# Graph result moved to channel order by TensorE selections into PSUM instead of DMA

## The reference, cut to what matters

```python
def _L2_conv_ref(x):                       # x already group-normalised
    X = x.reshape(Cs, N).T                 # nodes x 64 features
    A = (dist == 1) + eye
    sim = X @ X.T / (nrm[:, None] * nrm[None, :])
    m = (A + sim) * 0.5
    d = exp(diagonal(m) - logsumexp(m, axis=1))
    return relu(X * d[:, None])

def _L3_conv_ref(x, alpha, weight):
    a_bin = sign_ste(x - alpha[None])
    return conv2d(a_bin, sign_ste(weight), padding=1)      # 3 x 3, 64 -> 64

x = x + _L2_conv_ref(_gn(x))
x = x + _L3_conv_ref(_gn(x), alpha, weight)
```

## Time and profile before

| what | us |
|---|---|
| median of three runs | 321.22 |
| lowest and highest run | 321.09, 323.44 |
| the profiled execution's own time | 320.82 |
| its span, first to last instruction | 319.0 |
| TensorE busy in the span | 287.3 (90%) |
| VectorE busy | 270.7 (85%) |
| ScalarE busy | 167.6 (53%) |
| GpSimd busy | 119.3 (37%) |

### The profile page before, as it was taken

The page is one execution under the profiler, slowest core; times in us unless marked ns, Lnnn a source line. Parts: engine busy times, 40 slices in busy tenths (PEclk is TensorE's granted clock), DMA queues, the critical chain, the costliest instruction groups (busy, mean ns, idle before and its releaser), DMA issues.

```text
span 319.0 us, 6001 instructions
## 1 busy us (share of the span) xinstructions
PE 287.3 (90%) x2242; PEld 176.1 (55%) x2242; DVE 270.7 (85%) x415; ACT 167.6 (53%) x304; POOL 119.3 (37%) x163
## 2 busy tenths in 40 slices
PE   8698999599699999999999999479999999998895
PEld 8345988337354444567886644364344434367862
DVE  5799999797957599999988666976999999998673
ACT  1399553024250999940000004698888898999000
POOL 4004999982800669889996007000000000000000
PEclk9799999779799999999999999989999999999999
DMA  3421000000000000000000000363000000000603
GB/s 113 127 94 48 29 4 0 2 1 0 3 0 0 0 0 2 0 2 2 3 2 0 2 1 0 135 137 129 0 0 0 0 0 0 0 2 0 133 2 131
DMA packets 7613, 8.82 MB, mean 28 GB/s; under 512 B 2212, under 2 KB 5796, under 8 KB 7588
## 3 DMA queue, kind: packets, MB, share of 16 engines
q1 hardware_dynamic: 6260, 7.30, 7.5%
q10 hardware_dynamic: 1328, 1.18, 1.5%
HBM read 4.28 MB, written 2.10 MB: 20 GB/s over the span
## 4 chain that ended last, share of the span: by engine, by line
PE 64%; DVE 12%; issue 10%; ACT 8%; ACTq 3%; DMA 2%; DVEq 0%
PE ps L1376 15%; PE ps L1513 14%; PE ps L1390 9%; PE ps L1631 8%; PE ps L1527 6%; PE ps L1411 4%; ACT arena L891 3%; PE ps L1700 3%; ACT arena L874 2%; ACTq L389 2%; PE ps L1611 2%; DMA arena<-arena 2%; ACT arena L672 1%; DVE arena L1274 1%; DVE arena L1257 1%
## 5 line engine op out<-in xcount | busy, mean ns | idle before, releaser
L1631 PE MATMUL ps<-arena 128*128 (+1 forms) x256 | 63.3, 380 | 6.3 <-ACT arena L874 5.0
L874 ACT ACTIVATE arena<-ps 128x2048 f32<-128x2048 f32 x32 | 60.1, 1879 | 7.9 <-PE ps L1631 7.9
L1631 PEld LDWEIGHTS ps<-arena 128*128 (+1 forms) x256 | 24.3, 97 | 40.6 <-issue 14.1
L602 POOL TENSOR_TENSOR arena<-arena 128x768 f32<-128x768 f32 x21 | 40.1, 1940 | 4.8 <-ACT arena L777 4.6
L1257 DVE TENSOR_TENSOR arena<-arena 128x1024 f32 (+3 forms) x34 | 36.6, 1153 | 4.0 <-ACT arena L874 4.0
L1155 DVE TENSOR_TENSOR turns<-arena,ps 128x1024 f32<-128x1024 f32 x30 | 35.2, 1218 | 1.5 <-PE ps L1527 1.5
L1411 PE MATMUL ps<-ident 128*128 128x128 f32 x262 | 32.9, 287 | 3.3 <-DVE arena L1301 1.7
L1390 PE MATMUL ps<-arena 64*64 64x240 f32 (+3 forms) x576 | 31.2, 374 | 4.2 <-issue 2.6
L1376 PE MATMUL ps<-turns,k 128*128 128x512 f32 x80 | 34.8, 593 | 0.1
L1411 PEld LDWEIGHTS ps<-ident 128*128 128x128 f32 x262 | 31.9, 202 | 4.4 <-DVE arena L1301 1.9
L1513 PE MATMUL ps<-turns,shift 64*64 64x512 f32 x200 | 33.5, 592 | 0.0
(11 more groups left out here) (237 smaller groups left out, 506.6 us busy)
## 6 DMA issues: line engine op xcount, KB each, us to landing
scratch_x<-xs SPq DMA_DIRECT2D x4, 256.0 KB
arena<-arena SPq DMA_DIRECT2D x2, 512.0 KB, 3.3
out<-arena SPq DMA_DIRECT2D x4, 256.0 KB, 2.1
xs<-in_x SPq DMA_DIRECT2D x8, 64.0 KB
xs<-in_x ACTq DMA_DIRECT2D x8, 64.0 KB
arena<-arena SPq DMA_DIRECT2D x4, 128.0 KB, 3.4
arena<-arena ACTq DMA_DIRECT2D x4, 128.0 KB, 4.1
arena<-in_toep SPq DMA_DIRECT2D x1, 448.0 KB, 5.5
```

What stands on the lines that cost most here:

```text
L602: pool.tensor_tensor(out=view(folds[i % len(folds)], dx * 3 * PX, [(PX, 3), (1, PX)]), in0=view(hy, (by - dy) * W + (dy * 3 + dx) * PX, [( ...
L874: act.activation(E[k], ps[:, (k % 2) * 2048:(k % 2 + 1) * 2048], ACT.Exp, scale=0.5 / SPLIT ** 2, accum_out=rowsum[:, bass.ds(i, 1)]).then ...
L1631: ins = pe.matmul(bank(b0 + q), w, m[:, bass.ds(i * P + 512 * q, 512)], start=(t == 0), stop=(t == 1 and q > 0))
```

## The change

- `keep_nodes` uses Relu in place of Copy, so XT holds relu(X). The products xx, for the similarities, read the unrectified nodes from PSUM for all q.
- `scale_nodes` becomes one product of 1024 columns for each half. `add_back`, ScalarE's four scalings and the eight DMAs of `to_channels` go.
- A new `to_channels` on TensorE: for each half and each of two sources (x2R, then o2) 16 f32 matmuls, each with 32 columns of the identity (every fourth one, from t) as weights over all 128 partitions, 256 moving columns, and 32 partitions of PSUM as output. The two sources accumulate, so that x3 stands in channel order in two banks of each half: 0 and 1 for h=1, 2 and 3 for h=0. The addend's part is queued as soon as the far exponentials have left these banks; the other part waits for o2.
- The warm-up products between are replaced by 8 before the pair means of h=1; the 10 behind them stay.
- Statistics and signs read PSUM. The pair means move to bank 4+h and the convolution to banks 4 to 7.
- ScalarE moves each half of x3 from PSUM to x3S after the half's signs, for the last add, which waits for it.

```diff
-        o2, x3R = cut(0, 2048), cut(2048, 2048)
-
...
-        x3N = cut(16384, 2048)
+        o2, far_out = cut(0, 2048), cut(2048, 2048)
...
+        x3S = cut(16384, 2048)
...
+        def x3_bank(h, n=512):
+
+            return bank(2 * (1 - h), n)
+
+        def image_rows(b):
+
+            return view(x3_bank(b // 4), 64 * (b % 4), [(256, 4), (1, 64)])
...
-        def to_channels(eng, h, quarters):
-
-            for t in quarters:
-                eng.wait_ge(sem("x3_ready"), 4 * (1 - h) + t + 1)
-                eng.dma_start(view(x3N, h * 1024, [(256, 4), (1, 256)], 32 * t, 32),
-                              x3R[:, h * 1024 + t * 256:h * 1024 + (t + 1) * 256]).then_inc(sem(f"x3N_in{h}"), 16)
...
-            for h in (1, 0):
-                to_channels(sp, h, (0, 2))
...
-                act.activation(view(XT, q * 512, [(256, 2), (64, C4), (1, 64)]), nodes(ps, q), ACT.Copy).then_inc(sem("xt"), 1)
+                act.activation(view(XT, q * 512, [(256, 2), (64, C4), (1, 64)]), nodes(ps, q), ACT.Relu).then_inc(sem("xt"), 1)
...
-                    act.activation(x3R[:, c:c + P], ps[:, c:c + P], ACT.Exp, scale=0.5 / SPLIT ** 2,
+                    act.activation(far_out[:, c:c + P], ps[:, c:c + P], ACT.Exp, scale=0.5 / SPLIT ** 2,
...
-            act.wait_ge(sem("scale_ready"), 1)
-            for q in (3,):
-                for u in range(4):
-                    act.activation(o2[:, 256 * q + 64 * u:256 * q + 64 * u + 64], XT[:, 512 * q + 64 * u:512 * q + 64 * u + 64],
-                                   ACT.Copy, scale=Ssum[:, 4 * u + q:4 * u + q + 1]).then_inc(sem("scaled"), 1)
-            for h in (1, 0):
-                to_channels(act, h, (1, 3))
             for h in (1, 0):
                 root(rstd[:, 4 * h:4 * h + 4], pvar[:, 4 * h:4 * h + 4])
+                act.wait_ge(sem("apad"), 8 - 4 * h)
+                act.activation(x3S[:, 1024 * h:1024 * h + 1024], x3_bank(h, 1024), ACT.Copy).then_inc(sem("x3_kept"), 1)
...
                     dve.wait_ge(sem("xt"), q + 1)
-                    src = view(XT, q * 512, [(256, 2), (64, C4), (1, 64)])
-                else:
-                    src = nodes(ps, q)
-                dve.tensor_tensor(out=view(xx, q * 512, [(256, 2), (64, C4), (1, 64)]), in0=src,
+                dve.tensor_tensor(out=view(xx, q * 512, [(256, 2), (64, C4), (1, 64)]), in0=nodes(ps, q),
...
-            def scale_nodes(h, q, n):
-
-                dve.tensor_tensor(out=view(o2, h * 1024 + 256 * q, [(256, n), (64, 4), (1, 64)]),
-                                  in0=view(XT, h * 256 + 512 * q, [(512, n), (64, 4), (1, 64)]),
-                                  in1=view(Ssum, 16 * h + q, [(1, n), (4, 4), (0, 64)]), op=ALU.mult).then_inc(sem("o2_ready"), n)
-
-            def add_back(h, q):
-
-                c = h * 1024 + 256 * q
-                dve.scalar_tensor_tensor(out=x3R[:, c:c + 256], in0=o2[:, c:c + 256], scalar=0.0,
-                                         in1=view(x2R, h * 1024 + 64 * q, [(256, 4), (1, 64)]), op0=ALU.max,
-                                         op1=ALU.add).then_inc(sem("x3_ready"), 1)
+            def scale_nodes(h):
+
+                dve.tensor_tensor(out=view(o2, h * 1024, [(256, 4), (64, 4), (1, 64)]),
+                                  in0=view(XT, h * 256, [(512, 4), (64, 4), (1, 64)]),
+                                  in1=view(Ssum, 16 * h, [(1, 4), (4, 4), (0, 64)]), op=ALU.mult).then_inc(sem("o2_ready"), 1)
 
             def statistics(h, first, n):
 
-                dve.wait_ge(sem(f"x3N_in{h}"), 64)
+                dve.wait_ge(sem("x3_ready"), 2 - h)
                 for b in range(4 * h + first, 4 * h + first + n):
-                    dve.bn_stats(stats[:, 6 * b:6 * b + 6], image_rows(x3N, b)).then_inc(sem("moments"), 1)
...
-                link(dve.tensor_copy(pav, bank(h, 8)))
...
-                                      view(x3N, 1024 * h + 64 * b, [(256, 4), (16, 4), (1, 16)]), limit[:, b:b + 1], 0.5,
+                                      view(x3_bank(h), 64 * b, [(256, 4), (16, 4), (1, 16)]), limit[:, b:b + 1], 0.5,
...
-            dve.wait_ge(sem("x2R_in"), 16)
-            scale_nodes(1, 0, 1)
-            for q in range(4):
-                if q < 3:
-                    scale_nodes(1, q + 1, 1)
-                dve.wait_ge(sem("o2_ready"), q + 1)
-                add_back(1, q)
-            scale_nodes(0, 0, 3)
-            dve.wait_ge(sem("o2_ready"), 7)
-            for q in range(3):
-                add_back(0, q)
-            dve.wait_ge(sem("scaled"), 4)
-            add_back(0, 3)
+            scale_nodes(1)
+            scale_nodes(0)
...
                 dve.wait_ge(sem("l3_done"), i + 1)
+                dve.wait_ge(sem("x3_kept"), i // 2 + 1)
                 dve.tensor_tensor(out=view(yout, q * 512, [(PX, 2), (64, 4), (1, 64)]),
-                                  in0=view(x3N, 1024 * (q // 2) + 128 * (q % 2), [(64, 2), (256, 4), (1, 64)]),
-                                  in1=view(bank(2 + q), 0, [(PX, 2), (64, 4), (1, 64)]), op=ALU.add).then_inc(sem("y_ready"), 1)
+                                  in0=view(x3S, 1024 * (q // 2) + 128 * (q % 2), [(64, 2), (256, 4), (1, 64)]),
+                                  in1=view(bank(4 + q), 0, [(PX, 2), (64, 4), (1, 64)]), op=ALU.add).then_inc(sem("y_ready"), 1)
...
-                pe.matmul(bank(h, 8), pair_mean, mv[:, 8 * h:8 * h + 8], start=True, stop=False)
-                pe.matmul(view(bank(h), 1, [(2, 4)]), pair_mean, pstat[:, 4 * h:4 * h + 4], start=False,
+                pe.matmul(bank(4 + h, 8), pair_mean, mv[:, 8 * h:8 * h + 8], start=True, stop=False)
+                pe.matmul(view(bank(4 + h), 1, [(2, 4)]), pair_mean, pstat[:, 4 * h:4 * h + 4], start=False,
...
-            pe.wait_ge(sem("col_summed"), 5)
-            warm_up(14, 4)
-            for quarter in (2, 4, 6, 8):
-                pe.wait_ge(sem("x3_ready"), quarter)
-                warm_up(8, 4)
+            def to_channels(h, src, u, first):
+
+                for t in range(4):
+                    for q in range(4):
+                        ins = pe.matmul(view(x3_bank(h), 256 * t, [(1, 256)], 32 * q, 32), view(ident, t, [(4, 32)]),
+                                        view(src, 1024 * h + q * (64 if first else 256), [(u, 4), (1, 64)]),
+                                        start=first and t % 2 == 0, stop=not first and t % 2 == 1)
+                return ins
+
+            pe.wait_ge(sem("x2R_in"), 16)
+            pe.wait_ge(sem("far_exp"), 24)
+            to_channels(1, x2R, 256, True)
+            pe.wait_ge(sem("far_exp"), 32)
+            to_channels(0, x2R, 256, True)
+            pe.wait_ge(sem("col_summed"), 8)
+            for h in (1, 0):
+                pe.wait_ge(sem("o2_ready"), 2 - h)
+                to_channels(h, o2, 64, False).then_inc(sem("x3_ready"), 1)
+            warm_up(8, 6)
             pair_means(1)
-            warm_up(10, 4)
+            warm_up(10, 6)
             pe.wait_ge(sem("wsgn"), 3)
             pe.wait_ge(sem("warm"), warmed[0])
...
-                    ins = pe.matmul(bank(2 + q), wsgn[:, t * P:(t + 1) * P],
+                    ins = pe.matmul(bank(4 + q), wsgn[:, t * P:(t + 1) * P],
```

More of the change, by code:

```diff
@@ L252, in nodes @@
             return view(t, q * 512, [(1, 2), (P, C4), (2, 64)])
-        def image_rows(t, b):
-            return view(t, 1024 * (b // 4) + 64 * (b % 4), [(256, 4), (1, 64)])
+        def x3_bank(h, n=512):
+            return bank(2 * (1 - h), n)
+        def image_rows(b):
+            return view(x3_bank(b // 4), 64 * (b % 4), [(256, 4), (1, 64)])
         COL_PIECES = (16, 20, 24, 28, 0, 4, 8, 12)
@@ L1291, in _ @@
             dve.wait_ge(sem("scale_ready"), 1)
-            def scale_nodes(h, q, n):
-                dve.tensor_tensor(out=view(o2, h * 1024 + 256 * q, [(256, n), (64, 4), (1, 64)]),
-                                  in0=view(XT, h * 256 + 512 * q, [(512, n), (64, 4), (1, 64)]),
-                                  in1=view(Ssum, 16 * h + q, [(1, n), (4, 4), (0, 64)]), op=ALU.mult).then_inc(sem("o2_ready"), n)
-            def add_back(h, q):
-                c = h * 1024 + 256 * q
-                dve.scalar_tensor_tensor(out=x3R[:, c:c + 256], in0=o2[:, c:c + 256], scalar=0.0,
-                                         in1=view(x2R, h * 1024 + 64 * q, [(256, 4), (1, 64)]), op0=ALU.max,
-                                         op1=ALU.add).then_inc(sem("x3_ready"), 1)
+            def scale_nodes(h):
+                dve.tensor_tensor(out=view(o2, h * 1024, [(256, 4), (64, 4), (1, 64)]),
+                                  in0=view(XT, h * 256, [(512, 4), (64, 4), (1, 64)]),
+                                  in1=view(Ssum, 16 * h, [(1, 4), (4, 4), (0, 64)]), op=ALU.mult).then_inc(sem("o2_ready"), 1)
             def statistics(h, first, n):
-                dve.wait_ge(sem(f"x3N_in{h}"), 64)
+                dve.wait_ge(sem("x3_ready"), 2 - h)
                 for b in range(4 * h + first, 4 * h + first + n):
```

(4 more changed lines are left out.)

## The result

Four runs of each kernel, taken together: 322.29 us before (median), 317.32 after. The ratio is 0.9873 with a 95% interval of 0.9834 to 0.9912, so between 2.8 and 5.3 us less; predicted were 318.1 us, 3.1 less.

The account below looks back on a forecast made before the run. Bound: the chain of waits from the scale factors to the pair means, then TensorE's queue. Pair means move from 304.14 to 301.0, so span 319.0 - 3.1 = 315.9, execution 317.7, median 318.1 us; range 317.0 to 321.0.

Parts of the forecast that it names:

- rival A: TensorE's selection passes: four column groups at once, 0.053 us a pass; total 317.6 to 318.7 us; chance 0.71.
- D: Selection passes one at a time, 0.213 us each, 128 rows leaving room for one stream; total 337.6 us; chance 0.07.
- B: Selection passes with weight loads not hidden, 0.078 us each; gain 0.9, total 320.4 us; chance 0.09.
- C: Selection passes two at a time, strictly in order, 0.107 us each; 2.8 us slower, total 324.0 us; chance 0.08.
- The addend hidden: x2R selections on TensorE end at 295.0, 0.6 us before the first o2 selections, hidden under sums and first product.
- TensorE's queue as the new gate: Before the pair means: o2 selections and eight warm-ups hold them to 301.0, 1.2 us after VectorE is ready.
- Scale factors to pair means: Pair means begin about 6.7 us after the scale factors, right behind a warm-up product.
- Pair means to convolution: TensorE needs 3.05 us as before from pair means to convolution, warm-ups included.
- Signs from PSUM: First two sign images before the convolution: 0.02 us more each, margin 0.3, at most a tenth or so showing.
- ScalarE's moves: Two moves of 1024 columns out of PSUM, 1.03 us each, hidden with 1.0 and 1.5 to spare.
- The sum: Whole kernel: span 319.0 less 3.1 gives 315.9 us, median of the runs 318.1 us.
- Rival E: TensorE's clock falls; the 36 convolution passes cost 7.7 us more, total 325.8 us; chance 0.05.

Follow-up runs that it names:

- group_order: Changed kernel with the two selection loops exchanged, so eight passes of one column group stand together; one execution, 324.31 us.
- late_addend: Changed kernel with the addend's 64 passes queued behind the wait for the first scaled half: 322.83 us; `_warm` adds sixteen warm-up products in the gap: 321.35 us.
- no_eight: Changed kernel without the eight warm-up products before the pair means of h=1; ratio to the kernel before 0.9884.
- early_move: Changed kernel with ScalarE moving each x3 half out of PSUM before the root, signs reading that SBUF copy; ratio to the kernel before 0.9893.
- second set: The changed kernel itself timed again on another occasion, six runs: 318.16 us against 321.01 for the kernel before, ratio 0.9899.
- add_on_vector: Changed kernel with VectorE adding x2R to each scaled half and TensorE selecting the sum; one execution, 322.37 us.
- no_warm_ups: Changed kernel without both sets of warm-up products, before and after the pair means of h=1; one execution, 319.48 us.
- no_eight_early_move: Changed kernel without the eight warm-ups and with x3 moved to SBUF before the root for the signs; 316.61 us, ratio to the kernel before 0.9869.

## Why the prediction was right, point by point

- **Passes of the selections (rival A).** Forecast 0.053 a pass from the 64x64 tiles; measured 0.053 (64 in 3.69). A group of 32 columns over all 128 rows overlaps like a quadrant. One group by itself took 0.216 a pass (the last four starts of `group_order`, 304.73 to 305.38), as put for D from the earlier trace rows. Rivals B (0.078), C (0.107) and D (0.213) fell. The sentence of the Trainium skill (TensorE: Matmul & The Clock Gate, Part 3, The mechanism) that gave C, strict order of starts, is not borne out: pairs of passes in one group did not hold up the others, nor did four in a row, and in `group_order` passes started out of order (297.36 against 297.57). Nor is its rule on weight loads, by which column groups would never overlap theirs: 64 loads, 3.26 us from the first to the last, lay beside the passes.
- **The addend hidden.** Right, by 0.5 us rather than 0.6 (293.65 to the first pass of o2 at 294.13); `late_addend_warm` shows what it would cost without cover, 3.45.
- **TensorE's queue as the new gate.** Right in place and nearly in size: forecast 1.2 us behind VectorE, measured 1.4, and 1.23 recovered by `no_eight`.
- **Scale factors to pair means.** Forecast 6.7 us, measured 6.9 (292.73 to 299.64). The hand-over from VectorE to the selections took 0.14 (293.99 to 294.13) where 0.05 was put from the earlier trace rows; from there to the pair means it was 5.51 where 3.4 + 0.1 + 1.88 = 5.4 was put.
- **Pair means to convolution.** Forecast 3.05, measured 2.96.
- **Signs from PSUM.** The term that was mis-sized: 0.02 each was put, by the example of bn_stats; measured were 0.13 (482 ns against 352). The margin of 0.3 ahead of the convolution was used up: the two signs take 0.88 instead of 0.62, and the convolution starts 0.15 behind the second, a tie with the ten warm-ups that costs 0.02 at most (10.93 against 10.91 in `early_move`). That it cost no more was luck. Inside the convolution the late signs push the squares of h=0 back and cost 0.15. So the prediction's "at most a tenth or so" came out at 0.15 to 0.17, in a place it had not named. The bn_stats themselves did cost what was forecast, 420 ns against 414.

VectorE by line and shape in the changed kernel, columns as in the earlier trace rows:

```profile
L1317 DVE TENSOR_SCALAR turns<-ps,small 128x256 bf16<-128x256 f32 x8 | 3.3, 482 | 0.1
L1289 DVE BATCH_NORM_STATS2 stats<-ps 128x6 f32<-128x256 f32 x8 | 2.9, 420 | 1.1 <-PE ps L1661 1.1
```

- **ScalarE's moves.** Forecast 1.03 each with 1.0 to spare before the root and 1.5 before the third add; measured 1.02, with 0.72 and 1.05 to spare. No cost.
- **The sum.** Forecast 3.1 us; the two stretches give 2.99 - 0.15 = 2.84. The medians moved by 5.0 in the first set and by 2.85 in the second. 2.84 is the lower end of the first set's interval; in the profiled pair 1.6 us more was clock ahead of the change. Two of the four runs after (316.38 and 316.74) had a mean granted clock of 0.989 and 0.984, the other two (317.90 and 318.40) 0.973, the value of most runs in the second set. So it is the luck of the clock that puts 317.3 below 318.1; the second set's 318.16 is the fairer check.
- **Rival E, the clock.** It did not occur in the changed kernel. But `late_addend`, `add_on_vector` and `no_warm_ups` show that it was near, and the prediction priced only the gaps that the change leaves, not the work that fills them.

## What to carry to other kernels

A change of layout from rows to channels that waits for a DMA of nearly 5 us can be done in 1.7 us of TensorE's queue a half (2.0 until the last pass is over) by selections with columns of the identity, if the four column groups take turns in the queue after at most four passes. An addend that is known earlier can be put into PSUM first; here that cost no time and kept TensorE at work. When a wait goes, read the queue of the engine behind it: here products that only keep the clock up stood between the new work and the next step, and cost 1.2 of the 4.2 us that were to be had (`no_eight_early_move`). Then look for the next bound close behind: the slower signs had already caught up with the ten warm-ups. Price a change of a few us by a stretch between two landmarks in the trace, since the clock's grants in earlier stages move the total by 1.6 us between executions of the same code.

## What the runs showed of the hardware that I had not expected

- Four passes in a row of one column group overlap with the others at 0.055 us a pass, eight in a row run at 0.122. A pass of one group can start before a pass of another that stands ahead of it in the queue.
- A tensor_scalar of 256 columns from f32 to bf16 took 352 ns from SBUF and 482 ns from PSUM, while bn_stats of 256 columns took 414 and 420. So what an operand in PSUM costs must be read for each operation.
- After 4.4 us without work TensorE ran at a granted clock of 0.53 for the next 3.6 us, after 5.66 us at 0.55 for 6.6 us, and after 3.4 us with 0.61 busy at 0.50 for at least 2.3 us.
